# Three loads of a graph convolution moved from its last stage into the visits of groups 5 and 7, and the last stage reordered

## The chip, the cores and the metric

One core of one Trainium2 chip runs the whole program. The time is the device time of one execution in microseconds (us). Four engines compute: PE (TensorE: matmuls and transposes against an identity), DVE (VectorE), ACT (ScalarE) and POOL (GpSimd). SP only issues DMA transfers; ACT issues some too, from its own queue.

## The reference

`adj` is 4096 x 4096, `x` is 4096 x 128, all float32. The first layer takes `adj` as eigenvectors:

```
x_spec = adj.T @ x
h      = adj @ (exp(-evals * t)[:, None] * x_spec)
x1     = layernorm(x + h)
```

The second layer takes `adj` as a graph:

```
deg = rowsum(adj + I)
out = tanh(((adj + I) / deg) @ (x1 @ W) + b)
y   = layernorm(x1 + out)
```

So `adj` is needed three times: transposed, and then twice as it stands. The second use needs all of `x_spec`; the third needs x1 of the columns' rows.

## The kernel before, in words

`adj` is cut into 8 groups of 512 rows and 8 units of 512 columns. A load is one group by two units (a "wide"), 2 MB, fetched as four quarters, two issued by SP and two by ACT. Stage 1 reads all of `adj` once for `x_spec`. Stage 2 visits group after group and forms the spectral product, `adj` against `s`. When a group ends, its ending (a chain over PE, ACT, DVE and POOL) makes x1 and then `p = x1 @ W` for that group. From then on the unit with that group's number can be used for the graph product, `adj` against `p`. So a load of stage 2 whose units are already known serves both products; the units that were unknown at that visit have to be loaded again in stage 3, visit 8, for the graph product alone. These are 16 loads, in the order of the list `ORDER3`. The lists behind this are `LOADS2` (the 32 loads of stage 2) and `WORK`, the list of units in the order in which they are worked.

Every unit of a load is two steps (`STEP`), 200 in all. A step covers 256 columns of the matrix for 512 rows. It runs through the engines in this order, each engine going through the steps in the same order:

- DVE transposes it in blocks from the load's buffer into a slot of `vt` (`turn_step`, L596), two steps ahead; there are 6 slots (`RING`), and a slot is free when the matmuls of the step six before are done.
- If the step is in parts, ACT rounds it to `hi` (`hi_step`, L460), and POOL (L409) or DVE (`lo_step`, L603) takes `lo = vt - hi`. PE then makes three fast products for each of the two blocks and for each kind of product (L759, L760, L761): hi with hi, lo with hi, hi with lo.
- If the step is whole (`whole`), there is no hi and no lo, and PE multiplies the full float32 values (L755). These are the second steps of units 4 to 7 in visits 0 to 2 (spectral product) and in visit 8.

`on_vector` says which steps give their lo to DVE: in visits 3 to 7 each step whose number leaves 2 when divided by 4, in visit 8 every tenth step in parts. PE works on a step three positions after POOL (`LAG`). Endings are placed by positions counted from a group's last step (`since2`, `since3`): for instance POOL makes the inverse deviation at 4 (stage 2) or 5 (stage 3) behind it, and PE makes `x1 @ W` at 10.

There are 4 load buffers in stage 2 and 2 more in stage 3 (`late_raw`), which lie over the values of `s` and can be filled only when the last spectral product is done. At that position ACT issues the four quarters that are its share of these two loads. A load is issued when the last step of the load before it in that buffer (`BEFORE`) is transposed. The load with the last unit of an odd group is kept until the next even visit, since that unit becomes known only then. SP also issues the load of x for each group, and two transfers for the degrees, at loads named by `n % NU` and the like.

By this list visit 5 is steps 84 to 99, visit 7 steps 118 to 133 and stage 3 steps 134 to 199 (66 steps: 41 in parts, 25 whole). Groups end in stage 3 in the order 7, 0, 1, 6, 2, 5, 3, 4, with their last steps at 151, 155, 167, 171, 179, 187, 191 and 199.

Of the kernel before, what the change touches and what calls it, by code (L numbers as in the profile page):

```python
# [25 lines left out]


def spectral_then_graph_conv(nc, x, adj, evals, t, W, b, out):

# [18 lines left out]
    NG = N // (R * P)  # L50
    NK = N // CW
    JB = CW // P
    NU = NG // 2
    PAIRS = 2 * NK
    LAST = NG - 1
# [14 lines left out]
    def wides2(g):  # L70

        newest = (g - 1) // 2 if g else NU - 1
        known = [u for u in range(NU) if 2 * u + 1 < g and u != newest]
        unknown = [u for u in range(NU) if 2 * u + 1 >= g and u != newest]
        order = []
        while known or unknown:
            if unknown:
                order.append(unknown.pop(0))
            if known:
                order.append(known.pop(0))  # L80
        return order + [newest]


    ORDER3 = [(0, 0), (0, 1), (0, 2), (2, 1), (0, 3), (1, 1), (1, 2), (1, 3), (6, 3), (2, 2), (2, 3), (3, 2), (5, 3),
              (3, 3), (4, 2), (4, 3)]
    LOADS2 = [(g, u) for g in range(NG) for u in wides2(g)]


    WORK = []
    for n, (g, u) in enumerate(LOADS2):  # L90
        units = (2 * u + 1, 2 * u) if 2 * u + 1 == g else (2 * u, 2 * u + 1)
        for f in units:
            WORK.append((n, f, True, f < g, g))
            if n % NU == NU - 1 and g >= 2 and g % 2 == 0 and f == 2 * u:
                WORK.append((n - NU, g - 1, False, True, g))
    for i, (g, u) in enumerate(ORDER3):
        if i == 4:
            WORK.append((len(LOADS2) - 1, LAST, False, True, NG))
        for f in (2 * u, 2 * u + 1):
            WORK.append((len(LOADS2) + i, f, False, True, NG))  # L100
    NL = len(LOADS2) + len(ORDER3)
    LAST_STEP = [2 * max(i for i, w in enumerate(WORK) if w[0] == n) + 1 for n in range(NL)]
# [2 lines left out]
    LOADS = []  # L105
    END_OF_2 = 2 * max(i for i, w in enumerate(WORK) if w[2]) + 1
    free_at = {u: u - NU for u in range(BUFS)}
    for n, (g, u) in enumerate(LOADS2 + ORDER3):
        if n == len(LOADS2):
            free_at.update({u: END_OF_2 + RING for u in range(BUFS, BUFS3)})  # L110
        buf = min(free_at, key=free_at.get)
        LOADS.append(Load(g, u, buf))
        free_at[buf] = LAST_STEP[n]
# [83 lines left out]
    with ctx:  # L197
# [112 lines left out]
        def wait_buffer(eng, n):  # L310

            if LOADS[n].buf >= BUFS and BEFORE[n] is None:
                eng.wait_ge(mm_done, END2[LAST] + 1)
            elif BEFORE[n] is None:
                halves = range(4 * LOADS[n].buf, 4 * LOADS[n].buf + 4)
                wait_lo1(eng, max(q for q in halves if q in LATE_POOL))
                wait_lo1(eng, max(q for q in halves if q in LATE_DVE))
            else:
                eng.wait_ge(vturned, LAST_STEP[BEFORE[n]] + 1)

        def load_quarters(eng, n, quarters):
            ld = LOADS[n]
            for q in quarters:
                eng.dma_start(load_buffer(n)[q * QP:(q + 1) * QP].rearrange("p (a w) -> p a w", w=WQ),
                              adj_q[ld.group // 2, ld.group % 2, ld.wide, q]).then_inc(block_in[ld.buf], 16)
# [3 lines left out]
        @blk.sync  # L329
        def _(sp):  # L330
            def load1(src, k, freed=None, count=None):
                if freed is not None:
                    sp.compute_val(src.offset * 4)
                    sp.wait_ge(freed, count)
                sp.dma_start(raw[:, k], src).then_inc(raw_in[k], 16)

            def load_xn(v, par):
                sp.dma_start(xn[:, par, :], x_n[v]).then_inc(xn_in[par], 16)

            def visit1(v, par, v_index):  # L340

                for k in range(NK):
                    load1(adj_x[v_index, k], k, lo1_ready, (v - 1) * PAIRS + (2 * k + 2))
                    if k == 3 and par is not None:
                        sp.wait_ge(x_ready, v)
                        load_xn(v_index + 1, par)

            load_xn(0, 0)
            sp.dma_start(raw[:, 0, :R // 2], adj_x[0, 0][:, :R // 2]).then_inc(first_in, 16)
            sp.dma_start(raw[:, 0, R // 2:], adj_x[0, 0][:, R // 2:]).then_inc(raw_in[0], 16)  # L350
            for k in range(NK):
                if k:
                    load1(adj_x[0, k], k)
                if k == 3:
                    load_xn(1, 1)
            with sp.Fori(0, NU - 1) as d:
                visit1(2 * d + 1, 0, 2 * d + 1)
                visit1(2 * d + 2, 1, 2 * d + 2)
            visit1(LAST, None, LAST)

            for n in range(NL):
                wait_buffer(sp, n)
                load_quarters(sp, n, (0, 1))
                g = n // NU
                if n % NU == NU - 1 and g < NG:
                    sp.dma_start(x_sb[:, g, :], x_v[g // 2, g % 2]).then_inc(x_in[g % 2], 16)
                if n == 2 * NU - 1:
                    sp.wait_ge(deg_s, 3)
                    sp.dma_start(deg_by_tile, rdeg_tile[:, :, :]).then_inc(deg_out, 16)
                if n == 3 * NU - 1:  # L370
                    sp.wait_ge(deg_out, 16)
                    for h in range(NG):
                        sp.dma_start(rdeg[:, h, :], deg_by_group[h // 2, h % 2]).then_inc(deg_in, 16)
# [495 lines left out]
```

## Time and profile before

| what | value |
|---|---|
| time, median of 3 runs | 629.96 us (629.28 to 630.16) |
| the profiled execution, its own time | 632.82 us |
| its span, first to last instruction | 630.7 us |
| busy: PE, DVE, ACT, POOL | 590.4, 515.1, 396.3, 364.4 us |
| read from HBM | 172.13 MB |
| mean granted PE clock | 0.983 of full speed |

The span is cut by the stages: stage 1 and the turn to `s` to about 208 us, stage 2 to 500, stage 3 to 619, then the ending of the last group. "Busy" of PE overlaps, because matmuls are pipelined: the distance from one start to the next is what a matmul costs.

### The profile page before, as it was taken

The numbers are of one execution on the slowest core, as the hardware profiler recorded it, in microseconds if no ns is written. First come the engines' busy times: TensorE is split into PE (matmuls) and PEld (weight loads), VectorE is DVE, ScalarE is ACT, GpSimd is POOL, SyncE is SP. The second block draws the span as 40 slices with busy tenths as digits, with TensorE's granted clock in tenths as the row PEclk, the third lists the DMA queues.
The fourth block names the chain that finished last, engine by engine and source line by source line (L and its number), as shares of the span: only waits on it lengthen the run. The fifth ranks groups of instructions, "written<-read, shape, count | busy, mean of one in ns | idle before, by whom it ended". The sixth has DMA issues, their size and how long they took to land.

```text
span 630.7 us, 8071 instructions
## 1 busy us (share of the span) xinstructions
PE 590.4 (94%) x2486; PEld 451.3 (72%) x2486; DVE 515.1 (82%) x604; ACT 396.3 (63%) x859; POOL 364.4 (58%) x206
## 2 busy tenths in 40 slices
PE   6999999999996789999999999999999969999992
PEld 5878788778774566667888888888888847655561
DVE  4789989988887999698879889596776576989992
ACT  4899999999986644545565655545443454445552
POOL 0000000000131988877999999778886779796961
PEclk9999999999999799999999999999999989999997
DMA  8999999999999999999987999298994499999201
GB/s 285 386 387 386 386 387 387 387 387 387 386 331 328 280 301 252 287 266 272 317 220 198 263 280 302 60 264 204 247 251 133 128 346 296 345 332 296 58 18 50
DMA packets 141305, 174.67 MB, mean 277 GB/s; under 512 B 6868, under 2 KB 105428, under 8 KB 141272
## 3 DMA queue, kind: packets, MB, share of 16 engines
q1 hardware_dynamic: 88992, 121.68, 61.3%
q10 hardware_dynamic: 52280, 52.58, 30.6%
q8 instruction: 17, 0.28, 0.2%
q14 instruction: 16, 0.13, 0.1%
HBM read 172.13 MB, written 2.11 MB: 276 GB/s over the span
## 4 chain that ended last, share of the span: by engine, by line
PE 69%; POOL 9%; DVE 6%; ACT 5%; DMA 4%; issue 3%; SPq 1%; ACTq 1%; POOLq 0%; DVEq 0%
PE ps L759 13%; PE ps L761 13%; PE ps L760 13%; PE ps L735 7%; POOL lo L409 7%; PE ps L736 6%; PE ps L737 6%; PE ps L755 6%; DMA raw<-in_adj_dram 4%; ACT hi L445 3%; DVE vt L596 3%; PE ps L824 1%; PE ps L827 1%; POOL rstd L401 1%; ACT hi L460 1%
## 5 line engine op out<-in xcount | busy, mean ns | idle before, releaser
L409 POOL TENSOR_TENSOR lo<-vt,hi 128x1024 fp32r<-128x1024 f32 x129 | 326.7, 2559 | 59.1 <-ACT hi L460 58.2
L596 DVE STREAM_TRANSPOSE vt<-raw 128x1024 f32<-128x1024 f32 x184 | 222.2, 1226 | 62.9 <-PE ps L761 52.4
L460 ACT ACTIVATE hi<-vt 128x1024 fp32r<-128x1024 f32 x163 | 169.6, 1061 | 111.3 <-DVE vt L596 93.1
L579 DVE TENSOR_TENSOR lo<-raw,hi 128x1024 fp32r<-128x1024 f32 x124 | 153.5, 1240 | 21.3 <-ACT hi L445 20.7
L445 ACT ACTIVATE hi<-raw 128x512 fp32r<-128x512 f32 x256 | 158.2, 621 | 14.2 <-DMA raw<-in_adj_dram 4.8
L391 POOL TENSOR_TENSOR lo<-raw,hi 128x1024 fp32r<-128x1024 f32 x4 | 10.7, 2685 | 180.8 <-ACT hi L445 180.8
L759 PE MATMUL ps<-hi,s_hi 128*128 128x512 f32 x232 | 99.1, 427 | 9.5 <-issue 5.2
L735 PE MATMUL ps<-hi,xg_hi 128*128 128x512 f32 x256 | 102.0, 399 | 2.7 <-DVE lo L579 1.4
L736 PE MATMUL ps<-lo,xg_hi 128*128 128x512 f32 x256 | 99.9, 390 | 0.0
L737 PE MATMUL ps<-hi,xg_lo 128*128 128x512 f32 x256 | 99.8, 390 | 0.0
L759 PE MATMUL ps<-hi,p_hi 128*128 128x512 f32 x206 | 89.1, 433 | 7.0 <-POOL lo L409 7.0
L761 PE MATMUL ps<-hi,s_lo 128*128 128x512 f32 x232 | 91.6, 395 | 0.0
L760 PE MATMUL ps<-lo,s_hi 128*128 128x512 f32 x232 | 91.5, 394 | 0.0
L761 PE MATMUL ps<-hi,p_lo 128*128 128x512 f32 x206 | 81.3, 394 | 0.0
L760 PE MATMUL ps<-lo,p_hi 128*128 128x512 f32 x206 | 81.0, 393 | 0.0
L603 DVE TENSOR_TENSOR lo<-vt,hi 128x1024 fp32r<-128x1024 f32 x34 | 67.5, 1985 | 4.3 <-ACT hi L460 4.3
L755 PE MATMUL ps<-vt,full 128*128 128x512 f32 x148 | 69.5, 592 | 0.0
L759 PEld LDWEIGHTS ps<-hi,s_hi 128*128 128x128 f32 x232 | 44.3, 191 | 25.8 <-issue 9.3
L735 PEld LDWEIGHTS ps<-hi,xg_hi 128*128 128x128 f32 x256 | 48.0, 188 | 19.6 <-DVE lo L579 7.8
L759 PEld LDWEIGHTS ps<-hi,p_hi 128*128 128x128 f32 x206 | 39.2, 190 | 23.1 <-POOL lo L409 12.4
L737 PEld LDWEIGHTS ps<-hi,xg_lo 128*128 128x128 f32 x256 | 48.1, 188 | 10.3
L736 PEld LDWEIGHTS ps<-lo,xg_hi 128*128 128x128 f32 x256 | 48.1, 188 | 9.3
(66 smaller groups left out, 512.9 us busy)
## 6 DMA issues: line engine op xcount, KB each, us to landing
raw<-in_adj_dram SPq DMA_DIRECT2D x63, 1024.0 KB, 14.2
raw<-in_adj_dram SPq DMA_DIRECT2D x90, 512.0 KB, 9.3
raw<-in_adj_dram ACTq DMA_DIRECT2D x88, 512.0 KB, 11.6
late_raw<-in_adj_dram SPq DMA_DIRECT2D x8, 512.0 KB, 11.6
late_raw<-in_adj_dram ACTq DMA_DIRECT2D x8, 512.0 KB, 14.3
xn<-in_x_dram SPq DMA_DIRECT2D x8, 256.0 KB, 12.2
x_sb<-in_x_dram SPq DMA_DIRECT2D x8, 256.0 KB, 13.1
out_dram<-x_sb ACTq DMA_DIRECT2D x8, 256.0 KB, 3.0
```

What stands on the lines that cost most here:

```text
L409: nc.gpsimd.tensor_tensor(lo[:, slot(p), :], vt[:, slot(p), :], hi[:, slot(p), :].bitcast(f32), ALU.subtract).then_inc(pool_lo_ready, 1)
L445: last = nc.scalar.activation(hi[:, q % RING1, (r % 2) * CW:(r % 2 + 1) * CW], raw[:, k, r, :], ACT.Copy, accum_out=rsum[:, v, r * NK + k: ...
L460: nc.scalar.activation(hi[:, slot(s), :], vt[:, slot(s), :], ACT.Copy).then_inc(hi_ready, 1)
L579: nc.vector.tensor_tensor(lo[:, q % RING1, :], raw[:, k, 2 * h:2 * h + 2, :].rearrange("p r n -> p (r n)"), hi[:, q % RING1, :].bitcast(f3 ...
L596: nc.vector.transpose(vt[:, slot(s), :].rearrange("p (m a i) -> p m a i", m=2, a=RB), load_buffer(st.load).rearrange("p (a m e i) -> p e m ...
L735: nc.tensor.matmul(ps[:, k, :], xh, ah, start=first and r == 0, stop=False)
L736: nc.tensor.matmul(ps[:, k, :], xh, al, start=False, stop=False)
L737: last = nc.tensor.matmul(ps[:, k, :], xl, ah, start=False, stop=final and r == R - 1)
L755: return nc.tensor.matmul(out_t, full[:, STEP[s].unit - WHOLE_FROM, jj * C:(jj + 1) * C], vt[:, slot(s), jj * CW:(jj + 1) * CW], start=sta ...
L759: nc.tensor.matmul(out_t, vh, ah, start=start, stop=False)
L760: nc.tensor.matmul(out_t, vh, al, start=False, stop=False)
L761: return nc.tensor.matmul(out_t, vl, ah, start=False, stop=stop)
```

## The change

Three of the 16 loads of stage 3 are made earlier, for the graph product alone. Load (2, 1) (group 2, units 2 and 3) becomes the second load of visit 5; loads (2, 2) and (3, 2) (units 4 and 5 of groups 2 and 3) come second and fourth in visit 7. All of their steps are in parts: the four second steps of units 4 and 5, which `whole` took as whole in visit 8, are not whole in visit 7. Stage 3 has 13 loads left, in another order.

The visits are now steps 84 to 103 (visit 5: the new steps are 88 to 91), 122 to 145 (visit 7: the new steps are 126 to 129 and 134 to 137), and stage 3 is steps 146 to 199 (54 steps: 33 in parts, 21 whole). Groups end in stage 3 in the order 7, 0, 6, 2, 1, 3, 5, 4, with their last steps at 163, 167, 175, 183, 187, 191, 195 and 199. The number of steps, loads and matmul products is the same. Where the code counted loads by `n % NU`, it looks up the last load of a group in `LAST_LOAD`.

```diff
@@ -81,21 +82,33 @@
         return order + [newest]
 
 
-    ORDER3 = [(0, 0), (0, 1), (0, 2), (2, 1), (0, 3), (1, 1), (1, 2), (1, 3), (6, 3), (2, 2), (2, 3), (3, 2), (5, 3),
-              (3, 3), (4, 2), (4, 3)]
-    LOADS2 = [(g, u) for g in range(NG) for u in wides2(g)]
+    ORDER3 = [(0, 0), (0, 1), (0, 2), (4, 2), (0, 3), (1, 1), (6, 3), (1, 2), (2, 3), (1, 3), (3, 3), (5, 3), (4, 3)]
+
+    MIXED = {5: [(2, 1)], 7: [(2, 2), (3, 2)]}
+    LOADS2 = []
+    for g in range(NG):
+        mixed = list(MIXED.get(g, ()))
+        for u in wides2(g):
+            LOADS2.append((g, g, u))
+            if mixed:
+                LOADS2.append((g, *mixed.pop(0)))
+
+    LAST_LOAD = [max(n for n, (v, g, u) in enumerate(LOADS2) if g == v == h) for h in range(NG)]
 
 
     WORK = []
-    for n, (g, u) in enumerate(LOADS2):
+    for n, (v, g, u) in enumerate(LOADS2):
+        if v != g:
+            WORK.extend((n, f, False, True, v) for f in (2 * u, 2 * u + 1))
+            continue
         units = (2 * u + 1, 2 * u) if 2 * u + 1 == g else (2 * u, 2 * u + 1)
         for f in units:
             WORK.append((n, f, True, f < g, g))
-            if n % NU == NU - 1 and g >= 2 and g % 2 == 0 and f == 2 * u:
-                WORK.append((n - NU, g - 1, False, True, g))
+            if n == LAST_LOAD[g] and g >= 2 and g % 2 == 0 and f == 2 * u:
+                WORK.append((LAST_LOAD[g - 1], g - 1, False, True, g))
     for i, (g, u) in enumerate(ORDER3):
         if i == 4:
-            WORK.append((len(LOADS2) - 1, LAST, False, True, NG))
+            WORK.append((LAST_LOAD[LAST], LAST, False, True, NG))
         for f in (2 * u, 2 * u + 1):
             WORK.append((len(LOADS2) + i, f, False, True, NG))
     NL = len(LOADS2) + len(ORDER3)
@@ -105,7 +118,7 @@
     LOADS = []
     END_OF_2 = 2 * max(i for i, w in enumerate(WORK) if w[2]) + 1
     free_at = {u: u - NU for u in range(BUFS)}
-    for n, (g, u) in enumerate(LOADS2 + ORDER3):
+    for n, (g, u) in enumerate([(g, u) for v, g, u in LOADS2] + ORDER3):
         if n == len(LOADS2):
             free_at.update({u: END_OF_2 + RING for u in range(BUFS, BUFS3)})
         buf = min(free_at, key=free_at.get)
@@ -361,13 +374,13 @@
             for n in range(NL):
                 wait_buffer(sp, n)
                 load_quarters(sp, n, (0, 1))
-                g = n // NU
-                if n % NU == NU - 1 and g < NG:
+                if n in LAST_LOAD:
+                    g = LAST_LOAD.index(n)
                     sp.dma_start(x_sb[:, g, :], x_v[g // 2, g % 2]).then_inc(x_in[g % 2], 16)
-                if n == 2 * NU - 1:
+                if n == LAST_LOAD[1]:
                     sp.wait_ge(deg_s, 3)
                     sp.dma_start(deg_by_tile, rdeg_tile[:, :, :]).then_inc(deg_out, 16)
-                if n == 3 * NU - 1:
+                if n == LAST_LOAD[2]:
                     sp.wait_ge(deg_out, 16)
                     for h in range(NG):
                         sp.dma_start(rdeg[:, h, :], deg_by_group[h // 2, h % 2]).then_inc(deg_in, 16)
```

## Rows read from the trace of the kernel before

**Rows 1.** Stretches of visit 5, visit 7, stage 3 and its later part: stretch, us, busy time (instructions), clock, DMA.

```profile
374.30:412.50 38.20, 38.20 (x176) 31.41 (x175) 30.72 (x31) 20.08 (x27) 34.67 (x18) 1.00 0.70 198
...
456.00:500.10 44.10, 44.10 (x202) 36.16 (x200) 28.07 (x31) 20.68 (x29) 34.31 (x18) 1.00 0.59 161
...
500.10:618.70 118.60, 111.43 (x396) 71.18 (x394) 99.60 (x166) 57.48 (x86) 93.85 (x67) 0.99 0.82 238
519.97:618.73 98.76, 97.18 (x342) 60.96 (x342) 84.60 (x148) 48.78 (x75) 79.36 (x57) 1.00 0.77 218
```

**Rows 2.** PE in order of time, visit 5: start, us, what [idle before <-releaser].

```profile
374.29 0.39 PE L759 MATMUL ps<-hi,s_hi 128*128 128x512 f32 x1
...
375.65 0.39 PE L759 MATMUL ps<-hi,s_hi 128*128 128x512 f32 x1
...
380.24 0.40 PE L759 MATMUL ps<-hi,s_hi 128*128 128x512 f32 x1
...
382.98 0.39 PE L759 MATMUL ps<-hi,s_hi 128*128 128x512 f32 x1
```

**Rows 3.** PE in order of time, stage 3, the whole steps 187 and 189.

```profile
597.27 1.88 PE L755 MATMUL ps<-vt,full 128*128 128x512 f32 x4
...
600.37 1.88 PE L755 MATMUL ps<-vt,full 128*128 128x512 f32 x4
```

**Rows 4.** POOL in order of time, a narrow stretch of visit 5.

```profile
387.45 2.41 POOL L409 TENSOR_TENSOR lo<-vt,hi 128x1024 fp32r<-128x1024 f32 x1
```

**Rows 5.** POOL in order of time, visit 7.

```profile
461.44 5.59 POOL L409 TENSOR_TENSOR lo<-vt,hi 128x1024 fp32r<-128x1024 f32 x2 [0.22 <-ACT hi L460]
...
470.88 8.23 POOL L409 TENSOR_TENSOR lo<-vt,hi 128x1024 fp32r<-128x1024 f32 x3
483.71 4.74 POOL L409 TENSOR_TENSOR lo<-vt,hi 128x1024 fp32r<-128x1024 f32 x2 [4.60 <-ACT hi L460]
```

**Rows 6.** POOL in order of time, visit 5.

```profile
363.83 21.93 POOL L409 TENSOR_TENSOR lo<-vt,hi 128x1024 fp32r<-128x1024 f32 x8
...
387.45 12.84 POOL L409 TENSOR_TENSOR lo<-vt,hi 128x1024 fp32r<-128x1024 f32 x5
```

**Rows 7.** PE in order of time, visit 7, start of step 125.

```profile
475.59 0.39 PE L759 MATMUL ps<-hi,s_hi 128*128 128x512 f32 x1
```

**Rows 8.** DVE in order of time, visit 7, the lo of step 126.

```profile
471.59 2.78 DVE L603 TENSOR_TENSOR lo<-vt,hi 128x1024 fp32r<-128x1024 f32 x1
```

**Rows 9.** Order of time at the entry to stage 3, ACT's queue and PE.

```profile
499.84 6.53 ACTq L324 DMA_DIRECT2D late_raw<-in_adj_dram  x4
...
510.30 0.50 PE L759 MATMUL ps<-hi,p_hi 128*128 128x512 f32 x1 [3.65 <-POOL lo L409]
```

**Rows 10.** The chain that ended last, stage 3: start, us, what.

```profile
521.62 0.44 PE ps L818 x4
...
525.16 0.89 PE ps L824 x8
526.05 0.86 PE ps L827 x2
...
602.25 0.47 PE ps L834 x4
```

**Rows 11.** DVE in order of time, stage 3, parts of two endings and a transpose.

```profile
576.82 0.85 DVE L654 BATCH_NORM_STATS2 stats<-ps 128x6 f32<-128x128 f32 x4
...
578.00 1.21 DVE L596 STREAM_TRANSPOSE vt<-late_raw 128x1024 f32<-128x1024 f32 x1
579.13 1.09 DVE L687 SCALAR_TENSOR_TENSOR ps<-ps,rdeg,b_bc 128x128 f32<-128x128 f32 x4
...
582.42 0.67 DVE L693 TENSOR_TENSOR ps<-ps,x_sb 128x512 f32<-128x512 f32 x1
```

**Rows 12.** PE alone, stretches of 1.5 us: stretch, us, busy, clock, DMA.

```profile
221.00:222.50 1.50, 0.13 (x1) 1.00 1.11 293
...
511.50:513.00 1.50, 1.50 (x5) 0.50 1.10 346
```

## The prediction

> **What bounds the kernel now.** I read four views in this order: busy time by stretch, the order of time of PE and of POOL in visit 5, the same around visit 7, and the chain that ended last for stage 3. A "step" is one half of one unit. I numbered the 200 steps from the printed order of work and matched them to the trace by count, since each step has exactly one transpose, and one hi and one lo if it is in parts. Over the stretches of visit 5, visit 7 and stage 3 [rows 1] PE is busy without a hole in the first two and has 118.6 - 111.4 = 7.2 us of holes in the third. So in stage 2 the time is the number of matmuls, as long as the low parts arrive; in stage 3 it is not only that.
>
> Prices of a step on PE, start to start. In parts, one product: 374.29 to 375.65, 1.36 us. In parts, both products: 380.24 to 382.98, 2.7 us (2.72 as a rule) [rows 2]. A step in parts and the whole step behind it take 600.37 - 597.27 = 3.10 us together [rows 3]; the whole one is thus about 1.74, dearer for PE by 0.38 than one in parts, but free of ACT and POOL.
>
> Price on POOL: one lo is 2.41 us [rows 4]. Three of them with one DVE lo among them take 8.23 us [rows 5], so four steps of the stage 2 pattern (three on POOL, one on DVE) need 8.2 us of POOL. Against that PE needs 4 x 2.72 = 10.9 us for four steps with both products, but only 4 x 1.36 = 5.4 us for four with one. That is the one fact on which the forecast turns: both-product steps give POOL 2.7 us of lead per load, one-product steps take 2.8 away. Both new kinds of load are one-product, four steps, in parts.
>
> How much lead is there? In visit 5, little: POOL runs its lo operations back to back, 8 in 21.93 us from 363.83, then 1.6 us of the ending of group 4, then 5 more from 387.45, which end at 400.3 [rows 6]. Step 84, the first of visit 5, is on PE at 374.29, step 88 at 380.24 [rows 2], and the POOL operation for step 88 ended at about 380.1: a lead of 0.1 us. In visit 7 there is much: POOL waits 4.60 us before 483.71 [rows 5], and the low part of step 125 (the last of the two from 461.44) was there at 467.0 while PE came to it at 475.59 [rows 5, 7]: 8.6 us ahead.
>
> **The change, part by part.**
>
> (a) Load (2, 1) as second load of visit 5: steps 88 to 91. PE work +4 x 1.36 = 5.4 us. All up to step 87 is as before, and POOL's queue up to step 91 holds the same operations in the same places (DVE still takes steps 86 and 90). The lo of step 92 is the one at 387.45 and ends at 387.45 + 2.41 = 389.9 [rows 4]. Before, PE came to step 92 at 391.1 and didn't wait. Now steps 88 to 91 have one product each, so PE could be at step 92 at 380.24 + 5.4 = 385.7, but its operand is there at 389.9. PE waits 389.9 - 385.7 = 4.2 us, spread over steps 89 to 92. POOL can't be earlier: it has no hole between 363.8 and then, and its order is fixed. Bounds of this wait: 4.2 if nothing else moves; 0 if POOL were quicker than every row shows. I take 4.2. Behind step 92 there are eight both-product steps, in which POOL wins back its lead (8 x 0.67 us), so no second wait in visit 5. Cost of (a): 5.4 + 4.2 = 9.6 us.
>
> (b) Loads (2, 2) and (3, 2) in visit 7: steps 126 to 129 and 134 to 137. PE work +8 x 1.36 = 10.9 us. Four of these were whole steps before; in parts they ask for 4 more hi of ACT (idle more than half of this stretch [rows 1]) and 4 more lo (three or so of them POOL's), hidden in POOL's hole of 4.6 us and in the lead. With a lead over 5 us each block takes 2.8, and the four both-product steps between them give 2.7 back. What is late next: the DVE lo of step 130. Today step 126 holds that place, and its DVE lo ran 471.59 to 474.37 [rows 8]; PE would now be there near 472.9, and DVE some 1 us earlier, because the transpose ahead of it waits for a one-product step. Bounds 0 to 1.5 us; I take 0.5. If the lead were not there, it would cost up to 2 x 2.8 = 5.6 us. Cost of (b): 11.4 us.
>
> (c) DMA and queues: the three loads move with their 12 quarter loads, six in SP's queue and six in ACT's. Each load still waits for the load that held its buffer before to be transposed, some four loads back; the DMA share is 0.70 in visit 5 and 0.59 in visit 7 [rows 1], so there is room to land in time. SP's loads of x and of the degrees move with the last load of a group and are needed one ending later. Nothing, bounds 0 to 0.3 us.
>
> (d) Stage 3 loses 12 steps: four in parts of (2, 1) and, from (2, 2) and (3, 2), four pairs in part and whole. 4 x 1.36 + 4 x 3.10 = 17.8 us less on PE.
>
> (e) The entry to stage 3 stays: (0, 0), (0, 1), (0, 2) have eight steps in parts, and ACT is still held 6.53 us by issuing the quarters of the two late buffers [rows 9], which wait for the end of stage 2. The hole of 3.65 us on PE before step 138 [rows 9] stays. A DVE lo falls two steps earlier, POOL's count over these steps is the same. Nothing, bounds -1 to +1 us.
>
> (f) The new order of the rest. From 519.97 to 618.73 stage 3 has 25 pairs, 8 steps in parts and some other PE work: endings of group 7 0.44 + 0.89 + 0.86, the saved sum of group 1 put back, another full product in two records, 0.86, seven groups' transposes at 0.47 [rows 10]. 77.5 + 10.9 + 3.05 + 3.3 = 94.7; the stretch is 98.76 long [rows 1], so about 4.0 us of waits for low parts are in it. Some 1.4 of them lie at (1, 1), by its part in the stretch, and (1, 1) has four steps in parts in the new order too. Of the 20 pairs behind it with the other 2.6, six go away, while the endings stand closer (the last five groups end 8, 4, 4, 4 and 4 steps apart). Each ending asks DVE for 0.85 + 1.09 + 0.67 = 2.6 us [rows 11] beside four transposes a load. I take 0.4 us less waiting. Bounds: all 4.0 us of waits go (-4.0), or the close endings make DVE late (+2.6, one ending that nothing covers).
> Saved in stage 3: 17.8 + 0.4 = 18.2 us.
>
> The tail behind the last matmul (12 us from 618.7) is the ending of group 4 in both; the ending just ahead of it starts four steps, 6.2 us, earlier and is off DVE by then. Nothing.
>
> **Sum.** +9.6 + 11.4 - 18.2 = +2.8 us. The profiled execution took 632.82 us with a span of 630.7, which is 2.9 us over the median of 629.96; I add the difference to each: profiled 635.6 with a span near 633.5, median 632.8.
>
> Without any waits it would be +16.3 - 17.8 = -1.5 us: PE has less to do, because four whole steps turn into cheaper ones. The forecast says that the wait in visit 5 eats that and more.
>
> **Rivals.**
>
> The wait in visit 5 does not come (faster). Mechanism: the low parts for 89 to 92 are on time, because POOL's operations take less than now while DVE and ACT run further ahead. Against it: POOL has no hole from 363.83 to the ending and on to 400 [rows 6]. From 1.5 us of the 4.2 on that don't come, the result is no change; if all of it stays away, it is 632.8 - 4.2 = 628.6, and faster. Chance 0.14.
>
> The queue at (1, 1) and behind goes away in stage 3 (no change). (2, 1) is what drains POOL in stage 3 before (0, 3) and (1, 1); with it gone all 4.0 us of waits may go: 632.8 - 3.6 = 629.2. For it: POOL's load per step falls. Against: POOL already had time to recover before (1, 1). Anything from half of it on lands within 0.2% of before. Chance 0.19.
>
> Close endings bind DVE at the end of stage 3: 632.8 + 2.6 = 635.4. For it: four endings four steps apart, where a load gives PE 6.2 us and asks DVE for four transposes of 1.21 us [rows 11] and an ending of 2.6, 7.4 us. Against: the last four loads ask for 1.3 us more than they give each, which a lead of one ending covers twice, and the last two endings fall behind the last transpose. Chance 0.09.
>
> The clock. PE would stand still for about 1 us at a time four times in visit 5. In this trace the granted clock fell to 0.50 only behind the hole of 3.65 us (work before 506.7, none till 510.3), and stayed at 1.00 through 221.0 to 222.5 with 0.13 us of work [rows 12], so it should hold at 2.4 GHz. If it falls to 1.2 GHz as it did there, for two to three stretches like that of 511.5 to 513.0, PE loses half of 3 to 4 us, about 1.7 us: 634.5. Chance 0.05. The Trainium skill, TensorE: Matmul & The Clock Gate, section "A second HAM failure mode: psum-queue depth-cycling", says that frequent short idles between groups of matmuls make the clock swing and cost throughput; by that rule this rival would be the likely one and the time 634.5, by the rows the forecast is 632.8. No row here shows a swing from short idles.
>
> **How the numbers follow.** Forecast (wait of 3.4 to 5 us, stage 3 about as worked out) 0.53, with a range of its own of 631.3 to 634.3; a measurement of this kernel tells about 0.2%, 1.3 us, from no change. Faster 0.14; same 0.19 for its rival and 0.02 of the forecast's edge, 0.21; slower 0.51 + 0.09 + 0.05 = 0.65. The range 628.9 to 635.5 takes in the no-change rival, the forecast, DVE and the clock, and leaves out most of the faster rival and what lies above the dear ones.
>
> **What would show it.** Right: in visit 5 the PE starts of steps 88 to 92 stand some 2.4 us apart instead of 1.36, each idle ended by POOL's lo, and POOL shows the same back-to-back run; visit 5 is 9.6 us longer; visit 7 is 11 to 12 us longer with no PE holes and smaller POOL holes; stage 3's PE stretch is some 18 us shorter, with the hole of about 3.65 us at its start still there. Wrong: visit 5 longer by only 5.4 us; or stage 3 shorter by over 20 us; or PE waits for DVE's transposes in the last four loads; or a granted clock under 1.00 in visit 5.

## The result and the profile after

The changed kernel is slower. In the measurement of the change its median is 636.12 us (633.67 to 636.44, 4 runs) against 630.06 us, a ratio of 1.0084 with a 95% interval of 1.0057 to 1.0111. Measured a second time, beside other kernels, it is 634.17 us (6 runs) against 630.38 us, 1.0075 (1.0058 to 1.0092). The forecast was +2.8 us; measured are +3.8 to +6.1 us. The first median, 636.12 us, lies above the forecast's range of 628.9 to 635.5; the second lies inside it. The ten executions of the changed kernel fall into two groups: five at 633.6 to 634.2 us and five at 636.0 to 636.6. The first measurement caught one of the lower group in four, the second four in six. Single executions of one kernel lie up to 4.8 us apart here (e7, 628.71 to 633.47 us), which has to be kept in mind with every profile. Both profiles of the changed kernel are of the lower group. The profiled execution of before (span 630.7 us) was 2.4 us longer than that of a second profile of the same kernel (run e5, below, span 628.3 us), and I compare with that second one.

The stretches of visit 5, visit 6, visit 7 and stage 3 (columns as in [rows 1]), first of the changed kernel:

```profile
374.20:423.60 49.40, 46.00 (x200) 36.69 (x198) 35.90 (x36) 24.31 (x31) 42.90 (x20) 0.97 0.77 197
423.60:467.20 43.60, 43.60 (x200) 35.94 (x199) 32.16 (x33) 22.13 (x29) 35.22 (x17) 1.00 0.90 232
467.20:522.90 55.70, 55.15 (x248) 45.06 (x247) 40.88 (x41) 28.98 (x37) 50.51 (x24) 1.00 0.82 208
522.90:619.80 96.90, 90.57 (x332) 58.55 (x330) 83.30 (x148) 48.15 (x74) 75.86 (x56) 1.00 0.75 223
```

and the same four of the kernel before, second profile:

```profile
374.70:412.80 38.10, 38.10 (x175) 31.36 (x174) 28.63 (x31) 20.14 (x27) 34.69 (x18) 1.00 0.74 200
412.80:456.40 43.60, 43.60 (x199) 35.94 (x198) 34.34 (x33) 21.96 (x29) 34.84 (x18) 1.00 0.96 238
456.40:500.50 44.10, 44.10 (x202) 36.19 (x200) 28.10 (x31) 20.71 (x29) 34.34 (x18) 1.00 0.58 161
500.50:616.40 115.90, 109.01 (x396) 70.40 (x394) 99.44 (x166) 57.66 (x87) 94.56 (x67) 1.00 0.80 243
```

This is the whole account of the two profiled executions: visit 5 +11.3, visit 6 nothing, visit 7 +11.6, stage 3 -19.0, and the start of visit 5 is 0.5 us earlier: +3.4 us of span. That 0.5 us is scatter: visit 5 begins anywhere from 373.8 to 375.3 us in the profiles of these kernels. Forecast were +9.6, 0, +11.4 and -18.2. In visit 5 PE is idle for 49.4 - 46.0 = 3.4 us, where it had no hole before, and the clock is at 0.97.

PE in order of time in visit 5 (L772 is L759 of before), the rows that answer to [rows 2]:

```profile
380.10 0.40 PE L772 MATMUL ps<-hi,p_hi 128*128 128x512 f32 x1
...
382.31 0.50 PE L772 MATMUL ps<-hi,p_hi 128*128 128x512 f32 x1 [0.67 <-POOL lo L422]
...
385.65 0.50 PE L772 MATMUL ps<-hi,p_hi 128*128 128x512 f32 x1 [0.33 <-POOL lo L422]
...
389.70 0.50 PE L772 MATMUL ps<-hi,s_hi 128*128 128x512 f32 x1 [2.40 <-POOL lo L422]
...
391.55 0.63 PE L772 MATMUL ps<-hi,s_hi 128*128 128x512 f32 x1
...
394.50 0.48 PE L772 MATMUL ps<-hi,s_hi 128*128 128x512 f32 x1
```

Steps 88, 89, 91 and 92 start at 380.10, 382.31, 385.65 and 389.70. Four steps that are worth 5.44 us took 9.60: a wait of 4.2 us, every hole in it ended by POOL's lo. (The three holes add up to 3.4 us; the profile draws each matmul 0.39 us long where they follow one another every 0.23 us, so each hole is some 0.25 us longer by the starts than by the idle time.) The step behind it, 389.70 to 394.50, took 4.80 us; with its 0.36 of transposes it should take 3.08, and behind the same hole at the full clock it took 3.34 (e8, below). POOL has the same run as in [rows 6], moved by 0.15 us (the first row has one operation more in front):

```profile
361.33 24.27 POOL L422 TENSOR_TENSOR lo<-vt,hi 128x1024 fp32r<-128x1024 f32 x9
385.63 0.20 POOL L411 TENSOR_TENSOR veps<-mv,eps_sb 128x4 f32<-128x4 f32 x1
...
387.30 12.72 POOL L422 TENSOR_TENSOR lo<-vt,hi 128x1024 fp32r<-128x1024 f32 x5
```

The clock, stretches of 1.5 us of PE alone (columns as in [rows 12]):

```profile
388.30:389.80 1.50, 0.10 (x1) 1.00 1.14 259
389.80:391.30 1.50, 1.50 (x6) 0.82 1.10 228
391.30:392.80 1.50, 1.50 (x5) 0.50 1.05 259
392.80:394.30 1.50, 1.50 (x6) 0.54 1.07 260
394.30:395.80 1.50, 1.50 (x11) 1.00 1.13 331
```

Behind the hole of 2.40 us the granted clock went from 2.4 to 1.2 GHz, within step 92, and was back just before step 93 began at 394.50. That is the rival to which I gave 0.05.

In visit 7 PE has one hole, not before step 130 as I had said but before step 138, where DVE's lo is late:

```profile
503.31 0.50 PE L772 MATMUL ps<-hi,s_hi 128*128 128x512 f32 x1 [0.56 <-DVE lo L616]
```

### The profile page after: what moved, and what is told of

Same layout as the page of the kernel before. It is cut to its first block, busy times and chain, and to the rows that moved or that the text cites. A ratio compares the mean times of both kernels' runs of the same rounds, so it can differ in the third digit from the quotient of the medians.

```text
span 631.7 us, 8100 instructions
## 1 busy us (share of the span) xinstructions
PE 588.0 (93%) x2494; PEld 452.6 (72%) x2494; DVE 515.3 (82%) x606; ACT 401.1 (63%) x863; POOL 372.8 (59%) x208
## 4 chain that ended last, share of the span: by engine, by line
PE 56%; POOL 23%; DVE 6%; ACT 5%; DMA 4%; issue 3%; SPq 2%; ACTq 1%; POOLq 0%; DVEq 0%
POOL lo L422 19%; PE ps L772 9%; PE ps L774 9%; PE ps L773 9%; PE ps L768 7%; PE ps L748 7%; PE ps L749 6%; PE ps L750 6%; DMA raw<-in_adj_dram 4%; DVE vt L609 3%; ACT hi L458 3%; POOL rstd L414 1%; DVE lo L592 1%; PE ps L837 1%; ACT hi L473 1%
## 5 line engine op out<-in xcount | busy, mean ns | idle before, releaser
L422 POOL TENSOR_TENSOR lo<-vt,hi 128x1024 fp32r<-128x1024 f32 x131 | 334.6, 2581 | 53.2 <-ACT hi L473 52.3
L473 ACT ACTIVATE hi<-vt 128x1024 fp32r<-128x1024 f32 x167 | 174.4, 1061 | 118.6 <-DVE vt L609 94.3
L772 PE MATMUL ps<-hi,s_hi 128*128 128x512 f32 x232 | 99.5, 429 | 12.6 <-POOL lo L422 6.5
L772 PE MATMUL ps<-hi,p_hi 128*128 128x512 f32 x214 | 90.8, 424 | 7.3 <-POOL lo L422 7.3
L774 PE MATMUL ps<-hi,p_lo 128*128 128x512 f32 x214 | 84.1, 393 | 0.0
L773 PE MATMUL ps<-lo,p_hi 128*128 128x512 f32 x214 | 84.0, 393 | 0.0
L772 PEld LDWEIGHTS ps<-hi,s_hi 128*128 128x128 f32 x232 | 44.3, 191 | 29.5 <-POOL lo L422 11.3
L768 PE MATMUL ps<-vt,full 128*128 128x512 f32 x132 | 62.0, 592 | 0.0
L772 PEld LDWEIGHTS ps<-hi,p_hi 128*128 128x128 f32 x214 | 40.4, 189 | 21.8 <-POOL lo L422 10.7
L750 PEld LDWEIGHTS ps<-hi,xg_lo 128*128 128x128 f32 x256 | 48.1, 188 | 10.3
L749 PEld LDWEIGHTS ps<-lo,xg_hi 128*128 128x128 f32 x256 | 48.1, 188 | 9.3
## 6 DMA issues: line engine op xcount, KB each, us to landing
x_sb<-in_x_dram SPq DMA_DIRECT2D x8, 256.0 KB, 11.6
```

Source lines behind the costliest of these rows:

```text
L422: nc.gpsimd.tensor_tensor(lo[:, slot(p), :], vt[:, slot(p), :], hi[:, slot(p), :].bitcast(f32), ALU.subtract).then_inc(pool_lo_ready, 1)
L473: nc.scalar.activation(hi[:, slot(s), :], vt[:, slot(s), :], ACT.Copy).then_inc(hi_ready, 1)
L749: nc.tensor.matmul(ps[:, k, :], xh, al, start=False, stop=False)
L750: last = nc.tensor.matmul(ps[:, k, :], xl, ah, start=False, stop=final and r == R - 1)
L768: return nc.tensor.matmul(out_t, full[:, STEP[s].unit - WHOLE_FROM, jj * C:(jj + 1) * C], vt[:, slot(s), jj * CW:(jj + 1) * CW], start=sta ...
L772: nc.tensor.matmul(out_t, vh, ah, start=start, stop=False)
```

## The experiments

Each list below is against the source of the changed kernel; where two runs share a list, a comment names the run, and three dots or the text mark what is left out.

**e5, the kernel before once more**, for a second profile.

> The kernel before, profiled once more. Its first profiled execution had a span of 630.7 us, its other executions 627.0 to 629.7. Theory 2 (the difference between executions is made at the entry to stage 3, where ACT issues the quarters of the late buffers and the granted clock falls or not): all visits up to 7 as in the first profile within 0.3 us, and stage 3 shorter by about 2 us in its first ten steps. Rival: the difference lies in stage 1 or the start.

Measured: 630.45 us, span 628.3 us. Visits 5, 6 and 7 are as in [rows 1] to 0.1 us; stage 3 is 115.9 us instead of 118.6. The difference lies in stage 3, as theory 2 said, but only in part where it said: by the starts of the steps, 1.1 us of the 2.7 is in the first ten steps (all of it a longer wait before step 138), 0.7 at (1, 1), and the rest is in small waits behind it. In the first profile the clock fell at 511 [rows 12]; in this one, behind a hole of 2.55 us at the same step, it is at 1.00 through stage 3. That fall cost nothing: steps 138 and 139 took 5.65 us with it and 5.64 without, since PE waits for POOL's low parts there.

**e0, the changed kernel once more.**

> The changed kernel once more, as a yardstick for the others. Theory 1 (the wait for POOL in visit 5 and the fall of the granted clock behind it make it slower): about 636, and the profile again shows PE idle for some 2.4 us before step 92 and a granted clock of 0.50 behind it. Rival (the higher times of the first measurement are chance of a few executions): near 633.7, the time of its profiled execution.

Measured: 634.17 us (633.57 to 636.58, 6 runs), ratio 1.0075. Its profile repeats the first to 0.1 us in every visit, the low clock in step 92 included. Four of the six lie near 634 and two near 636, so the rival was right that the first three high times were in part chance; the loss of some 4 us remains. In this profile the clock fell a second time, behind a hole of 2.40 us before step 150, and stage 3 was no longer for it: 96.9 us, step 154 starting 18.6 us into it as in the first profile.

**e4, PE kept busy through the wait.** Steps 88, 90 and 91 are followed by matmuls whose result is thrown away.

```diff
+    FILL = {88: 3, 90: 2, 91: 10}
...
                 last.then_inc(mm_done, 1)
+                for _ in range(FILL.get(s, 0)):
+                    nc.tensor.matmul(ps[:, 6, :], s_hi[:, :C], s_hi[:, :CW], start=True, stop=True)
```

> The changed kernel with 3, 2 and 10 more matmuls on PE behind steps 88, 90 and 91, into a bank that is not in use yet, so that PE is busy while it waits for the low parts; their result is thrown away. Theory 1, its clock part: the granted clock stays at 1.00 through steps 92 and 93, and the time is 1.5 to 2.5 us below that of the changed kernel in the same call. Rival (the clock costs nothing, since POOL sets the pace there): the same time within 0.5 us.

Measured: 634.19 us, ratio 1.0067 (1.0051 to 1.0083), against 634.17 for e0. Its visit 5 as a stretch:

```profile
374.80:422.90 48.10, 47.94 (x215) 38.54 (x214) 36.03 (x36) 24.31 (x31) 43.02 (x20) 1.00 0.80 203
```

The clock stays at 1.00 and visit 5 is 1.3 us shorter than with the low clock, so the local price is shown. The gain of 1.5 to 2.5 us that I expected in the whole was not measured: the medians are equal. With six executions each from two groups some 2 us apart they could hide 1.3 us, so they don't show that the clock costs nothing either. The two profiles differ by 0.5 us of span: e4's visit 5 is 1.3 us shorter but begins 0.6 us later, and its stage 3 is 0.1 us longer, though the clock fell there, during step 150.

**e1 and e2, one part of the change each**, stage 3 in the old order without the moved loads (the `ORDER3` of each is left out of the list).

```diff
-    MIXED = {5: [(2, 1)], 7: [(2, 2), (3, 2)]}
+    MIXED = {5: [(2, 1)]}                      # e1
+    MIXED = {7: [(2, 2), (3, 2)]}              # e2
...
-        if i == 4:
+        if i == 3:                             # e1 alone
```

> Only load (2, 1) is moved, to visit 5; stage 3 keeps the old order without it. Theory 1: visit 5 is some 11 us longer than before (5.4 of matmuls, 4.2 of waiting for low parts, 1.7 of low clock), stage 3 is 5.4 us shorter plus 1 to 2 us of its waits: 634 to 635, so this part alone is the whole loss. Rival (visit 5 hides it and the loss is made in visit 7 or by the new order): 629 to 630.5.

> Only loads (2, 2) and (3, 2) are moved, to visit 7; stage 3 keeps the old order without them. Theory 1: visit 7 is 11 to 12 us longer, stage 3 is 12.4 us shorter plus up to 1.5 us of waits: 628 to 629.5, a little faster than before. Rival (the parts in visit 7 cost waits as well): 631 to 633.

Measured: e1 638.83 us, ratio 1.0132 (1.0117 to 1.0147); e2 634.56 us, 1.0065 (1.0049 to 1.0082). Both are above what I expected, e1 by 3.8 us and e2 by over 5 us, and e2's time is that of neither theory. The visits are not to blame: e1's visit 5 is 49.5 us, e2's visit 7 is 55.8, just as in the changed kernel, and visit 7 of e1 is 44.0. What went wrong is stage 3, whose row for e2 is

```profile
512.20:621.60 109.40, 101.36 (x356) 65.97 (x354) 88.53 (x157) 53.41 (x82) 87.53 (x64) 0.95 0.77 219
```

109.4 us, where 115.9 - 12.4 = 103.5 would be the old stage less the removed steps. Two side effects of my own edits were in it. First, which low parts go to DVE in stage 3 hangs on a running count of steps in parts, and every removed or moved step shifts it. In the kernel before DVE takes the eighth step of stage 3, in the changed one the sixth, in e1 the fourth, in e2 only the eleventh, so that in e2 POOL had one more operation in its queue at the entry, where PE waits for each, and the clock fell twice there (0.95 over the stage). Second, in e1 I had put the last unit of group 7 one load too early.

**e6 and e7, the same with DVE's turn held at the eighth step.**

```diff
-            return SPLIT_COUNT[s] % 10 == 0
+            return (SPLIT_COUNT[s] - SPLIT_COUNT[145]) % 10 == 0      # e6; 149 in e7
```

> As e1 (only load (2, 1) moved, to visit 5), but the count that gives every tenth low part in stage 3 to DVE is shifted, so that it falls on the eighth step of stage 3 as in the kernel before. In e1 the first ten steps of stage 3 lost 3 us or more against the changed kernel, and theory 2 says that this comes from where DVE takes its low part: 1 to 3 us below e1's 638.8, so 636 to 638. Rival (it comes from removing (2, 1) itself): as e1.

> As e2 (only loads (2, 2) and (3, 2) moved, to visit 7), with the low part of DVE on the eighth step of stage 3 as in the kernel before. Visit 7 costs 11.7 and stage 3 has 12.4 us less to do; theory 2: 629 to 631, 3 to 5 us below e2's 634.6, so that the part in visit 7 is neutral. Rival (visit 7's part loses by itself): as e2, 634.

Measured: e7 629.87 us (12 runs), ratio 0.9995 (0.9981 to 1.0009), 4.7 us below e2 (the two from different measurements), with this stage 3:

```profile
511.90:616.20 104.30, 96.90 (x356) 62.74 (x354) 89.21 (x157) 53.32 (x82) 86.67 (x64) 1.00 0.76 229
```

So the part in visit 7 is neutral: +11.7 in the visit, -11.6 in stage 3. Of the 5.1 us between this stage 3 and e2's, 4.2 lie in its first ten steps, where the one moved low part is. For e6 the expectation failed: 640.26 us (5 runs), 1.0156 (1.0138 to 1.0173), 1.4 us above e1. In the profiles its first eleven steps of stage 3 are 2.5 us shorter than e1's, but the whole stage only 1.5 (113.9 us against 115.4). Both lose 2.6 us at the twelfth step, where PE waits for p of group 7 for the misplaced unit. Why e6's executions are not faster than e1's stays open, and (2, 1) moved alone with that unit in its place was not run.

**e8 and e9, all three loads moved, stage 3 in the old order.**

```diff
-    ORDER3 = [(0, 0), (0, 1), (0, 2), (4, 2), (0, 3), (1, 1), (6, 3), (1, 2), (2, 3), (1, 3), (3, 3), (5, 3), (4, 3)]
+    ORDER3 = [(0, 0), (0, 1), (0, 2), (0, 3), (1, 1), (1, 2), (1, 3), (6, 3), (2, 3), (5, 3), (3, 3), (4, 2), (4, 3)]
-        if i == 4:
+        if i == 3:                                  # e8 alone
```

> All three loads moved as in the change, but stage 3 in the old order without them. My prediction gave the order nothing much: within 1 us of the changed kernel's 634.2. Rival, from the profiles: the waits for low parts behind the fifteenth step of stage 3 fell from about 3.9 to 1.7 us, and the order did that: 1.5 to 2.5 us above the changed kernel, near 636.

> As e8 (all three loads moved, stage 3 in the old order), with the last unit of group 7 back in its place four loads into stage 3. In e8 and e1 I had it one load earlier, and PE waited 2.0 us there for the low part of p of group 7, with a fall of the clock behind it. Without this: about 635 to 636, 1 to 2 us above the changed kernel's 634.2, if the new order is worth what the profiles show; within 0.5 us of 634.2 if my prediction's 'order gives nothing much' holds.

Measured: e8 638.71 us, 1.0122 (1.0102 to 1.0142); e9 636.44 us, 1.0093 (1.0079 to 1.0108). PE of e8 in order of time shows the misplaced unit:

```profile
552.12 0.47 PE L772 MATMUL ps<-hi,p_hi 128*128 128x512 f32 x1 [2.01 <-DVE p_lo L689]
```

p of group 7 is not ready three loads into stage 3, and PE waits 2.01 us for it. (The clock fell behind this hole; behind the holes of 2.00 and 2.01 us at the same place in e1 and e6 it did not.) In e9 this is gone. Stage 3 of e9 and, for the clock, visit 5 of e8:

```profile
523.90:623.70 99.80, 91.89 (x332) 58.49 (x330) 84.56 (x153) 49.70 (x78) 78.16 (x60) 1.00 0.77 219
```

```profile
375.20:423.30 48.10, 44.77 (x200) 35.74 (x200) 35.99 (x36) 24.33 (x31) 43.02 (x21) 1.00 0.79 205
```

e9's stage 3 is 2.9 us longer than the changed kernel's 96.9, at a clock of 1.00 in both. The two run alike for seventeen steps, then e9 waits more, so in these two profiles the new order is worth 2.9 us. Three things weaken this. The order also moves DVE's second low part from the 23rd to the 21st step of stage 3. The changed kernel's own order took 99.3 us in e10 and e11, below. And in the medians it is 2.3 us against the second measurement of the changed kernel (636.44 - 634.17), 0.3 against the first, 1.4 against all ten of its executions, with intervals of the ratios that overlap. So the order gains something in the profiles; how much of the time it is worth is not shown. And e8's visit 5, step for step the one of the changed kernel and with the same 3.3 us of holes, got through them without a fall of the clock: 48.1 instead of 49.4 us.

**e10 and e11, (2, 1) elsewhere.** (The second number of an entry in `MIXED` is the load; the first says behind which load of the visit it comes, counted from 0.)

```diff
-        mixed = list(MIXED.get(g, ()))
-        for u in wides2(g):
+        mixed = dict(MIXED.get(g, ()))
+        for i, u in enumerate(wides2(g)):
             LOADS2.append((g, g, u))
-            if mixed:
-                LOADS2.append((g, *mixed.pop(0)))
+            if i in mixed:
+                LOADS2.append((g, *mixed[i]))
...
+    MIXED = {5: [(2, (2, 1))], 7: [(0, (2, 2)), (1, (3, 2))]}      # e10
+    MIXED = {6: [(2, (2, 1))], 7: [(0, (2, 2)), (1, (3, 2))]}      # e11
```

> The changed kernel with one difference: load (2, 1) comes behind the third load of visit 5, where POOL is 5 to 6 us ahead, instead of behind the first, where it is 0.1 us ahead. Theory 1: the wait of 4.2 us and the clock's 1.7 us go, visit 5 costs 5.4 to 6 us over before instead of 11.3, and the time is 628 to 629.5. Rival (a one-product load in visit 5 costs its wait wherever it stands, since POOL is behind all through the visit): 632 to 634.

> The changed kernel with load (2, 1) behind the third load of visit 6 instead of in visit 5. In the profile before, POOL was 5 us ahead there. Theory 1: visit 5 as before (38.2 us), visit 6 5.4 to 6.5 us longer, 628 to 629.5. Rival: visit 6 keeps one load for the next visit, so only three buffers turn over, and a load comes late: 630 or more.

Measured: e10 630.89 us, ratio 1.0002 (0.9987 to 1.0017); e11 630.51 us, 0.9989 (0.9975 to 1.0003). Visits 5 and 6 of e10:

```profile
374.50:418.10 43.60, 43.60 (x199) 35.86 (x198) 35.31 (x36) 24.43 (x31) 40.19 (x20) 1.00 0.88 218
418.10:462.70 44.60, 43.97 (x200) 35.91 (x199) 33.94 (x33) 22.05 (x29) 39.55 (x19) 1.00 0.94 232
```

and of e11:

```profile
375.30:413.50 38.20, 38.20 (x176) 31.38 (x175) 28.73 (x31) 20.07 (x27) 34.79 (x18) 1.00 0.72 203
413.50:462.50 49.00, 49.00 (x223) 40.42 (x222) 39.73 (x38) 26.48 (x33) 41.84 (x21) 1.00 0.96 246
```

The same load with the same steps costs 11.3 us as second in visit 5, 5.5 + 1.0 as fourth in visit 5, and 5.4 as fourth in visit 6, which is its matmuls and nothing else. That shows the cause: not the load, but the lead of POOL at its place. By counting the operations in the traces, POOL was 0.2 us ahead of PE at step 88 of the changed kernel, 6.2 at the new load's first step in e10 and 5.5 at the same point of visit 6 in the kernel before. In e10 six steps with one product then follow one another and use the lead up to 0.3 us, and the 1.0 us in visit 6 is a hole of 0.63 us ended by POOL's lo. In e11's visit 6 PE has no hole, so the late load of the rival did not come, although the time fell in the rival's range. The times came out 1 to 2 us above my 628 to 629.5. In the profiles stage 3, the same list of steps as in the changed kernel, took 99.3 us in both and not 96.9. PE of e11 in stretches of 1.5 us at the entry to stage 3:

```profile
536.00:537.50 1.50, 0.57 (x2) 0.84 1.10 347
537.50:539.00 1.50, 1.50 (x5) 0.50 1.11 348
539.00:540.50 1.50, 1.50 (x7) 0.53 1.10 348
```

The clock fell there, behind a hole of 2.34 us before step 154, and this time it cost 1.6 us, since POOL was not what PE waited for next. Most of the rest is a wait before step 172, a hole of 0.54 us ended by POOL's lo.

**e12, e11 with one more low part for DVE in that queue.**

```diff
-            return SPLIT_COUNT[s] % 10 == 0
+            return SPLIT_COUNT[s] % 10 == 0 or s == 153
```

> As e11 ((2, 1) in visit 6), and DVE takes the low part of one more step, 153, in the queue at the entry to stage 3. There POOL works off steps 150, 152, 153 and 154 one behind the other while PE waits 2.3 us before step 154. Theory (POOL's queue sets that stretch): POOL has one operation of 2.4 us less in it, steps 150 to 158 are 2 to 3 us shorter, the clock doesn't fall there, 627 to 628.5, faster than before by 0.3 to 0.5%. Rival (DVE is as full there, with its transposes and the ending of group 7): as e11, 630.5.

Measured: 629.92 us, ratio 0.9990 (0.9974 to 1.0007): no gain that can be told from e11 or from before. Steps 150 to 158 were not 2 to 3 us shorter but 0.6 us longer than in e11, and the clock fell twice in them. POOL of e12 in order of time:

```profile
523.39 5.67 POOL L422 TENSOR_TENSOR lo<-vt,hi 128x1024 fp32r<-128x1024 f32 x2 [4.03 <-ACT hi L473]
531.97 0.20 POOL L411 TENSOR_TENSOR veps<-mv,eps_sb 128x4 f32<-128x4 f32 x1 [2.91 <-DVE mv L673]
```

POOL's operation was saved, and POOL then waited 2.91 us for DVE's aggregates of group 7's ending, which stand behind the extra lo on DVE. The rival is right for this place. No version was measured faster than the kernel before beyond the interval.

## Why the prediction was right, and where its terms were off

Direction and mechanism held: PE waits in visit 5 for POOL's low parts. The closeness of the number is in part luck, since terms that were off have opposite signs (visit 5 +1.7, visit 7 +0.2, stage 3 -0.8), and the first measurement's median lies outside the range. Of the prediction's own signs of being wrong one came true, a granted clock under 1.00 in visit 5, and two of its signs of being right did not: the steps 88 to 91 are not 2.4 us long each, and no hole of 3.65 us stands at the start of stage 3 but one of 2.41. Taking its terms in order:

- Load (2, 1) in visit 5: the wait of 4.2 us is measured as 4.2, step 92 starts at 389.70 against the 389.9 worked out from the one POOL row [rows 4], and e10 and e11 take it away by moving the load to where POOL has a lead. My statement of its spread was off: the four steps took 2.21, 1.49, 1.85 and 4.05 us, with 0.67, 0.33 and 2.40 us of idle time, not four times 1 us. That mattered, since the clock fell behind the one hole of 2.40 us. I had argued from a trace without a PE hole between 1.65 and 3.65 us in stages 2 and 3, which could not say what a hole of 2.40 does; and the 3.65 was not the only hole with a low clock, as I wrote, for it was low from 203.5 us on too, around the hole of 5.17 us before stage 2. The Trainium skill, TensorE: Matmul & The Clock Gate, section "A second HAM failure mode: psum-queue depth-cycling", has short idles making the clock swing; the trace agrees in part: of the six profiles with this hole of 2.40 us (the changed kernel's, e0, e1, e6, e8, e9) it fell behind it in five, and not in e8. The holes of 0.67 and 0.33 us brought no fall in any of them. The price is 49.4 - 48.1 = 1.3 us, a term that the sum lacked and that I had put at 1.7 in a rival of chance 0.05.
- Loads (2, 2) and (3, 2) in visit 7: +11.4 forecast, +11.6 measured. The small wait of 0.5 us is there as 0.56, at step 138 instead of 130.
- DMA, the retained unit and the tail: nothing, as said.
- The order of stage 3: this is the mis-sized term. I took 0.4 us less waiting; stage 3 fell by 19.0 instead of 18.2, that is 1.2 us less waiting. If the 2.9 us between the profiles of e9 and the changed kernel are the order's, keeping the old order would have added waits that I had taken as unchanged; I had no ground for that beyond the even spread of the old waits. The 4.0 us of waits from which I started were also high: by the same sum the second profile of the kernel before has 2.3 us and the changed kernel 1.3. Against the first profile, from which the forecast was made, stage 3 is 21.7 us shorter, more than the 20 us that I had named as a sign of being wrong; 2.7 of these are what that first execution was longer.
- The entry of stage 3: I had a DVE lo fall two steps earlier and took nothing for it. For the changed kernel the bound of 1 us held, but e2 against e7 shows that the place of this one operation can be worth 4 to 5 us, with the falls of the clock that came with it.

Measured, the visits give 11.3 + 11.6 - 19.0 = +3.9, less the 0.5 us by which visit 5 began earlier: +3.4 us, the difference of the spans, and close to the +3.8 of the second measurement. Of the no-change rival, that the waits in stage 3 go away, 1.0 us happened (2.3 to 1.3). The faster rival (no wait in visit 5) and the one with close endings on DVE did not happen: in stage 3 no PE hole of the last four loads names DVE. The medians of the first measurement differ by 6.1 us and those of the second by 3.8 because they caught the two groups in different shares; what stays open is what makes the groups. The executions of the changed kernel have spans either of 631.2 to 632.2 or of 633.5 to 634.6 us, those of e11 either 625.5 to 626.4 or 628.5 to 629.5. A fall of the clock more or less would give such a step, and e11's profiled execution, one of the upper ones, has one; no profile of a lower one of e11 was taken, nor one of an upper one of the changed kernel, so this is argued and not shown.

## What to carry to other kernels

Work that is moved under other work has to be weighed against the engine that feeds the bottleneck, at the very place where it goes: read how far that engine is ahead there, and how many microseconds per step it gains or loses. The same load cost 11.3 us with a lead of 0.1 to 0.2 us, and its bare 5.4 us with a lead of 5.5. And take two profiles of the kernel before: these two were 2.4 us apart, nearly the whole of the forecast. Where an assignment hangs on a running count (each tenth step, each fourth), every edit of the order shifts it: hold it fixed when you test one part, or you measure the shift, as e1 and e2 did.

## What the runs showed of the hardware

The granted clock of PE falls behind holes that are much shorter than the 3.65 us of [rows 9], and not each time. Behind 2.40 us of idle before step 92 it fell to 0.50, at the same hole in e8 it stayed at 1.00; behind 2.34 us in e11 it fell, behind 2.32 us at the same step of the changed kernel it did not. Over visits 5 to 7 and stage 3 of all fourteen profiles there are 26 holes of 2.26 to 2.75 us; it fell behind 15 of them. What a fall costs depends on what PE waits for next: 1.3 us in visit 5 and 1.6 at step 154 of e11, but nothing behind the first long hole of stage 3 (before, e0 and e4), where PE then waited for POOL in any case.
